# Layer 1's softmax pass of a graph network on one core: all feature weighting and a quarter of the copying out on GpSimd, the per-head scales in PSUM

## The reference, cut to what matters

```python
h = (x @ W_lin + b_lin).reshape(N, HEADS, EMB)
ee = (edge_attr @ W_edge + b_edge).reshape(-1, HEADS, EMB)
x_i = h[src]
x_j = h[dst] + ee
alpha = (x_i * att_i).sum(-1) + (x_j * att_j).sum(-1)
alpha = jnp.where(alpha >= 0, alpha, NEG_SLOPE * alpha)
amax = jax.ops.segment_max(alpha, src, num_segments=N)
e = jnp.exp(alpha - amax[src])
denom = jax.ops.segment_sum(e, src, num_segments=N)
alpha = e / (denom[src] + 1e-16)
messages = x_j * alpha[:, :, None]
out = jax.ops.segment_sum(messages, src, num_segments=N)
```

## Time and profile before

| what | value |
|---|---|
| median of 3 runs | 10118.95 us (10105.5 to 10135.94) |
| the profiled execution | 10148.2 us, span 10146.4 us |
| DVE busy over the span | 6640.8 us, 65% |
| ACT busy over the span | 4732.1 us, 47% |
| POOL busy over the span | 6862.4 us, 68% |
| the pass that is changed, first to last record | 4650.8 to 5342.9 us |

### The profile page before, as it was taken

One profiled execution on the slowest core, in us unless ns is written; L12 is line 12 of the kernel. 1 busy time (PEld: TensorE's weight loads), 2 busy tenths in 40 slices (PEclk: granted clock), 3 DMA queues, 4 the chain that ended last, 5 costly groups with the idle time before them and its releaser, 6 DMA issues. The chain is left out here.

```text
span 10146.4 us, 93449 instructions
## 1 busy us (share of the span) xinstructions
PE 2857.7 (28%) x19432; PEld 2389.4 (24%) x19432; DVE 6640.8 (65%) x9437; ACT 4732.1 (47%) x6635; POOL 6862.4 (68%) x6738
## 2 busy tenths in 40 slices
PE   1112587873000000000003566666664400000002
PEld 1111477773000000000003344444443200000002
DVE  7888777775122232226994688888886677777775
ACT  1111477772121111115991577777774344444442
POOL 6767777775677777775443777777775277777774
PEclk9999877775555555555556677777776655555555
DMA  3332322222233332324662444444442477777773
GB/s 103 101 94 89 87 72 80 76 92 32 95 120 112 105 116 102 116 98 181 261 249 63 114 140 134 140 134 140 134 140 77 150 237 236 236 237 236 236 237 104
DMA packets 722785, 1395.94 MB, mean 138 GB/s; under 512 B 409551, under 2 KB 439452, under 8 KB 715094
## 3 DMA queue, kind: packets, MB, share of 16 engines
q0 software_dynamic: 287072, 587.19, 21.1%
q1 hardware_dynamic: 406786, 639.32, 18.9%
q10 hardware_dynamic: 28852, 168.65, 4.6%
HBM read 827.48 MB, written 602.51 MB: 141 GB/s over the span
## 5 line engine op out<-in xcount | busy, mean ns | idle before, releaser
L823 POOL DMA_INDIRECT l_rows<-in_x,l_idx x1568 | 1638.1, 1045 | 685.5 <-issue 446.8
L2484 POOL DMA_INDIRECT l_rows<-table,l_idx x1568 | 1485.8, 948 | 660.8 <-issue 471.8
L1964 POOL DMA_INDIRECT l_rows<-h,l_idx x1568 | 1528.1, 975 | 571.3 <-issue 445.0
L1304 POOL DMA_INDIRECT rows<-l_rows,l_idx x1568 | 1503.6, 959 | 524.5 <-issue 496.5
L1999 PE MATMUL l_made<-l_kv_w,l_rows_t 128*128 128x256 f32 x3136 | 1081.3, 501 | 768.0 <-ACT l_kv L2029 452.6
L2560 ACT ACTIVATE l_lifted<-l_rows,l_up 128x256 f32<-128x256 f32 x1568 | 639.5, 460 | 1031.3 <-DMA l_rows<-table,l_idx 1031.3
L1999 PEld LDWEIGHTS l_made<-l_kv_w,l_rows_t 128*128 128x128 f32 x3136 | 753.3, 257 | 971.4 <-issue 842.7
L1260 ACT COPY l_rows<-l_run 128x1792 f32<-128x1792 f32 x56 | 191.6, 3421 | 1561.5 <-POOLq L88 1520.8
L1293 DVE TENSOR_TENSOR l_rows<-l_run,l_weights_ps 128x56 f32<-128x56 f32 x56 | 12.0, 215 | 1296.5 <-POOLq L88 1296.2
L1737 PE MATMUL l_wide<-l_diag,l_ones 128*128 128x384 f32 x4 | 3.3, 928 | 2957.3 <-DVEq L1767 2957.3
L1737 PEld LDWEIGHTS l_wide<-l_diag,l_ones 128*128 128x128 f32 x4 | 1.0, 311 | 2958.2 <-DVEq L1767 2958.2
(11 more groups left out here) (400 smaller groups left out, 12352.7 us busy)
## 6 DMA issues: line engine op xcount, KB each, us to landing
sums<-l1s_out ACTq DMA_DIRECT2D x56, 1988.0 KB, 6.6
sums<-l_out SPq DMA_DIRECT2D x112, 924.0 KB, 4.4
spread<-zeros SPq DMA_DIRECT2D x28, 3612.0 KB, 12.7
l_spread<-spread SPq DMA_DIRECT2D x112, 903.0 KB
l1s_rows<-rows SPq DMA_DIRECT2D x56, 1008.0 KB, 6.1
spread<-zeros SPq DMA_DIRECT2D x56, 938.0 KB
l_spread<-spread SPq DMA_DIRECT2D x56, 938.0 KB, 10.9
sums<-l_out ACTq DMA_DIRECT2D x56, 896.0 KB
```

The source lines that it names most:

```text
L823: pool.indirect_dma_start(rows[:, b, t], None, a["x"], bass.IndirectOffsetOnAxis(ap=idx[:, b, t:t + 1], axis=0)) \
L1304: pool.indirect_dma_start(g["rows1_d"], bass.IndirectOffsetOnAxis(ap=idx[:, b, t:t + 1], axis=0), rows[:, b, t], None).then_inc(sent[b], 16)
L1964: pool.indirect_dma_start(rows[:, c.r, t, 0:C], None, g["h2_d"], bass.IndirectOffsetOnAxis(ap=idx[:, c.r, t:t + 1], axis=0)).then_inc(got[ ...
L2484: pool.indirect_dma_start(rows[:, b, t], None, g["table3_d"], bass.IndirectOffsetOnAxis(ap=idx[:, b, t:t + 1], axis=0)) \
```

## The change

In `source_order_sums`:

- `weigh` on POOL (now L1508) does all 140 columns of a half, as two tensor_tensor instructions of 70 x 28 elements (L1513), into the SBUF tensor that held scales and weighed values before. It waits for the exponentials and for `scanned[n]` of the chunk before; `begun` is gone.
- `copy_out` on POOL (L1518) is new: it copies the last 35 of the 140 sums of a half into `outb` (L1521). ACT copies the other 105 (L1560).
- DVE's `sums` keeps only a column copy of 140 elements (L1490, from SBUF to SBUF) and two scans of 2030 elements, one for each head (L1496).
- The scales of each head lie in a PSUM tensor of their own, written by ACT once for each half and head (L1554), with semaphores `scale_ready` and `scale_used`.
- `scores` is unchanged, and so are SP's loads (the count they wait for is raised by one engine, not two) and the stores, which now also wait for POOL's copy.

```diff
-        LOW = F // 2
-        weighed_low = s.ps("l1s_weighed_low", [P, 2 * 512])[:, 0:LOW * (T + 1)].rearrange("p (f t) -> p f t", t=T + 1)
-        scale_high = s.ps("l1s_scale_high", [P, 6 * 512])[:, 0:(W - LOW) * (T + 1)].rearrange("p (f t) -> p f t", t=T + 1)
+        COPIED = W * 3 // 4
+        scale_ps = [s.ps(f"l1s_scale{h}", [P, 4 * 512])[:, 0:F * (T + 1)].rearrange("p (f t) -> p f t", t=T + 1) for h in range(H)]
+        weighed, run_all = scale, run[:].rearrange("p n h f t -> p n (h f) t")
...
                 def sums(c):
-                    b = c.b
-                    wait(v, exp_ready[b], c.h + 2)
                     for n in range(PARTS):
-                        at = slice(n * T, (n + 1) * T)
-                        v.tensor_tensor(weighed_low[:, :, 1:].rearrange("p f t -> p t f"), rows[:, b, at, 0:LOW],
-                                        exp[:, b, 1, 0, at].unsqueeze(2).to_broadcast([P, T, LOW]), ALU.mult).then_inc(rows_used[b][n], 1)
-                        v.tensor_copy(weighed_low[:, :, 0], run_all[:, 1 - n, 0:LOW, T]).then_inc(begun, 1)
-                        wait(v, low_ready[n], c.at + 1)
+                        wait(v, weighed_ready[n], c.at + 1)
+                        v.tensor_copy(weighed[:, n, :, :, 0], run[:, 1 - n, :, :, T])
                         wait(v, copied[n], c.at + 1)
+                        wait(v, out_copied[n], c.at + 1)
                         v.drain()
...
+                        for h in range(H):
+                            wait(v, scale_ready[h], c.at * PARTS + (n + 1))
+                            last = v.tensor_tensor_scan(run[:, n, h].rearrange("p f t -> p (f t)"), scale_ps[h].rearrange("p f t -> p (f t)"),
+                                                        weighed[:, n, h].rearrange("p f t -> p (f t)"), 0.0, ALU.mult, ALU.add)
+                            last.then_inc(scale_used[h], 1)
+                        v.drain().then_inc(scanned[n], 1)
...
                 def weigh(c, n):
                     at = slice(n * T, (n + 1) * T)
                     wait(pool, exp_ready[c.b], c.h + 2)
-                    if not (isinstance(c.g, int) and c.at == 0 and n == 0):
-                        wait(pool, begun, c.at * PARTS + n)
...
+                    wait(pool, scanned[n], c.at + 1)
+                    for h in range(H):
+                        last = pool.tensor_tensor(weighed[:, n, h, :, 1:].rearrange("p f t -> p t f"), rows[:, c.b, at, 0:F],
+                                                  exp[:, c.b, 1, h, at].unsqueeze(2).to_broadcast([P, T, F]), ALU.mult)
+                    last.then_inc(rows_used[c.b][n], 1)
+                    pool.drain().then_inc(weighed_ready[n], 1)
+
+                def copy_out(c, n):
+                    wait(pool, scanned[n], c.at + 2)
+                    wait(pool, stored[n], (c.at + 1) * 16)
+                    pool.tensor_copy(outb[:, n, :, COPIED:W].rearrange("p t w -> p w t"), run_all[:, n, COPIED:, 1:])
+                    pool.drain().then_inc(out_copied[n], 1)
+
+                def turn(c, after):
+                    copy_out(c, 0)
+                    if after:
+                        weigh(after, 0)
+                    copy_out(c, 1)
+                    if after:
+                        weigh(after, 1)
...
-                def low(c, n):
...
-                def high(c, n):
...
+                def scales(c, n, h):
+                    wait(act, scale_used[h], c.at * PARTS + (n + 1))
+                    nc.scalar.copy(scale_ps[h][:, :, 1:], exp[:, c.b, 0, h, n * T:(n + 1) * T].unsqueeze(1).to_broadcast([P, F, T])).then_inc(scale_ready[h], 1)
...
-                    nc.scalar.copy(outb[:, n, :, 0:W].rearrange("p t w -> p w t"), run[:, n].rearrange("p h f t -> p (h f) t")[:, :, 1:])
+                    nc.scalar.copy(outb[:, n, :, 0:COPIED].rearrange("p t w -> p w t"), run_all[:, n, 0:COPIED, 1:])
...
                 def turn(c, after):
-                    high(c, 1)
+                    scales(c, 1, 0)
+                    scales(c, 1, 1)
                     if after:
                         exponentials(after)
                     store(c, 0)
+                    send(c, 0)
                     if after:
-                        low(after, 0)
-                        high(after, 0)
+                        scales(after, 0, 0)
+                        scales(after, 0, 1)
                     store(c, 1)
-                    if after:
-                        low(after, 1)
+                    send(c, 1)
```

More of the change, by code:

```diff
@@ L1435, in source_order_sums @@
         rows_used = [two(f"rows_used{b}_") for b in range(2)]
-        low_ready, high_ready, scanned, copied, stored = (two(n) for n in ("low_ready", "high_ready", "scanned", "copied", "stored"))
-        set_up, begun, high_weighed = sem("l1s_set_up"), sem("l1s_begun"), sem("l1s_high_weighed")
+        scanned, copied, out_copied, stored, weighed_ready = (two(n) for n in ("scanned", "copied", "out_copied", "stored", "weighed_ready"))
+        set_up, scale_ready, scale_used = sem("l1s_set_up"), two("scale_ready"), two("scale_used")
         flat = lambda t: t.rearrange("p h t -> p (h t)")
@@ L1444, in _ @@
                     for n in range(PARTS):
-                        wait(sp, rows_used[c.b][n], (c.h + 1) * 2)
+                        wait(sp, rows_used[c.b][n], c.h + 1)
                         sp.dma_start(rows[:, c.b, n * T:(n + 1) * T].rearrange("p t w -> p (t w)"),
@@ L1454, in _ @@
                     for n in range(PARTS):
-                        v.sem_inc(rows_used[b][n], 2)
+                        v.sem_inc(rows_used[b][n], 1)
                     v.sem_inc(exp_ready[b], 1)
@@ L1458, in _ @@
                     v.sem_inc(copied[b], 1)
+                    v.sem_inc(out_copied[b], 1)
                     v.sem_inc(stored[b], 16)
-                v.memset(scale_high, 0.0)
+                    v.sem_inc(scale_used[b], 1)
+                    v.memset(scale_ps[b], 0.0)
                 v.drain().then_inc(set_up, 1)
@@ L1522, in weigh @@
-                    pool.drain().then_inc(high_weighed, 1)
-                pool.wait_ge(set_up, 1)
-                for r in range(UNROLL):
[L1526 to L1531, removed]
+                    wait(pool, scanned[n], c.at + 1)
+                    for h in range(H):
+                        last = pool.tensor_tensor(weighed[:, n, h, :, 1:].rearrange("p f t -> p t f"), rows[:, c.b, at, 0:F],
+                                                  exp[:, c.b, 1, h, at].unsqueeze(2).to_broadcast([P, T, F]), ALU.mult)
@@ L1533, in _ @@
+                pool.wait_ge(set_up, 1)
+                weigh(Chunk(0, 0), 0)
+                weigh(Chunk(0, 0), 1)
+                with pool.Fori(0, NB // UNROLL - 1) as q:
+                    for r in range(UNROLL):
+                        turn(Chunk(q, r), Chunk(q, r + 1) if r + 1 < UNROLL else Chunk(q + 1, 0))
+                for r in range(UNROLL):
+                    turn(Chunk(NB // UNROLL - 1, r), Chunk(NB // UNROLL - 1, r + 1) if r + 1 < UNROLL else None)
             @block.scalar
@@ L1557, in store, with send @@
                     wait(act, stored[n], (c.at + 1) * 16)
-                    nc.scalar.copy(outb[:, n, :, 0:W].rearrange("p t w -> p w t"), run[:, n].rearrange("p h f t -> p (h f) t")[:, :, 1:])
+                    nc.scalar.copy(outb[:, n, :, 0:COPIED].rearrange("p t w -> p w t"), run_all[:, n, 0:COPIED, 1:])
                     nc.scalar.copy(outb[:, n, :, W:W + H], top[:, c.r, :, at].rearrange("p h t -> p t h")).then_inc(copied[n], 1)
+                def send(c, n):
                     wait(act, copied[n], c.at + 2)
+                    wait(act, out_copied[n], c.at + 2)
                     act.dma_start(sums_v[:, bass.ds((c.at * PARTS + n) * wide, wide)], outb[:, n].rearrange("p t w -> p (t w)")).then_inc(stored[n], 16)
                 exponentials(Chunk(0, 0))
-                low(Chunk(0, 0), 0)
-                high(Chunk(0, 0), 0)
-                low(Chunk(0, 0), 1)
+                scales(Chunk(0, 0), 0, 0)
+                scales(Chunk(0, 0), 0, 1)
                 def turn(c, after):
-                    high(c, 1)
+                    scales(c, 1, 0)
+                    scales(c, 1, 1)
                     if after:
```

15 lines of the change are left out of this document (removed).

## The result

| | before | changed |
|---|---|---|
| median | 10127.44 us (4 runs, 10105.5 to 10151.37) | 10312.84 us (4 runs, 10295.15 to 10317.21) |
| ratio | | 1.0175, 95% interval 1.015 to 1.02 |
| the profiled execution | 10148.2 us | 10317.21 us |

What follows compares the result with a forecast made beforehand. DVE was taken to set the pace at 23.80 us a chunk. 26 x 7.6 for held scores, +8 and -5 at the edges gave +201 us; put onto the median, 10320 us (+2.0%), range 10215 to 10400.

Steps and rivals of the forecast that it cites:

- clean period: Time a chunk in the changed pass if DVE waited for nobody: 21.8 to 21.9 us.
- C: Duration of POOL's new copy of 980 elements a half, taken as 1.9 us.
- T: End of a chunk's second scans, when POOL's second burst is let go and DVE goes on to the scores.
- What the first burst leaves over: POOL work let go by the first half's end and still running when the second scans end: 0.8 us.
- The hold: In the scores, POOL instructions make DVE's SBUF operations wait one by one; period 31.4 us against 23.8, +7.6 a chunk.
- how many of the twelve score instructions pass POOL's gaps: One DVE instruction, perhaps two, passes each gap; about four of twelve done at T + 10.5, scores ending at T + 13.1.
- The sign of being wrong: If score lines 1468 to 1471 keep 0.16 to 0.24 us, the mechanism is wrong.
- The edges: Start and end of the pass: +8 us up to and after the first sums, -5 us at the last chunk.
- Rival 1: Score operations with two tensor inputs are not held: 2.8 us less a chunk, -73, 10247 us; chance 0.18.
- Rival 2: No hindrance of weight at a steady pace, clean period of 21.8 holds: faster, 10062 us; chance 0.10.
- Rival 3: Three or more DVE instructions pass each gap: +0.7 to +3 us a chunk, 10137 to 10197 us; chance 0.07.
- Rival 4: POOL's copy is far from 1.9 us: at 1.0, 10276 us; at 4.1, 10434; no separate chance given.

Runs made afterwards that it cites:

- e2_fence_18: Kernel of e1_fence with POOL copying out 18 of the 140 columns instead of 35, ScalarE 122; ratio to the kernel before 0.9969.
- e1_fence: Changed kernel plus one wait: POOL starts its second burst of a chunk only after VectorE's scores are done; ratio to the kernel before 0.9991.
- e4_spare_tt: Kernel before plus one POOL tensor_tensor of 1960 elements on a spare tensor during each chunk's scores; 11654.88 us against 11560.83 for the kernel before.
- e5_spare_set: e4_spare_tt with the extra POOL instruction made a memset of 3920 elements; 10136.30 us against 10150.98 for the kernel before.
- e3_no_pool_copy: Changed kernel without POOL's copy, ScalarE copying all 140 columns, no wait added; 11729.31 us against 11560.83 for the kernel before.
- e6: e2_fence_18 plus a wait at the pass's start: POOL's second-half weighting follows chunk 1's scores; ratio to the kernel before 0.9972.

## Why the prediction was right, and where it was off

The direction, the mechanism and the bound were right. That 10320 lies within 8 us of the measured 10312.84 is in part luck: +201 was forecast, the medians are 185 apart and the profiled executions 169, and the median of the kernel before had moved up by 8 us with a fourth run.

- **The bound and the clean period.** DVE set the pace, and the sum of its own work gave 21.8 to 21.9 us a chunk. e2_fence_18, where POOL is nearly out of the way, has 22.16.
- **What moved to POOL and what it takes.** C was taken as 1.9 us and is 1.92; two weightings in 7.5 are 7.45. POOL's burst was to end at T + 10.5, and it ends at T + 10.57 (4987.11 - 4976.54). What the first burst leaves over was put at 0.8 and is 0.64. Its path was only half right: the first burst's weightings follow POOL's copy, which ends at 4969.40, but also wait for the exponentials, which end in the same moment (the `<-ACT l1s_exp L1549` at 4969.76). So a shorter copy would not have shortened what is left over.
- **The hold.** It was read from two rows at the beginning of the pass. The steady pace of the changed kernel, e1_fence (taken away by time alone) and e4_spare_tt (put into the kernel before) show it. The forecast stated the rule with POOL instructions that read SBUF; for copies that was too narrow, since a memset held one as well (e4_spare_tt, e5_spare_set).
- **The term that was mis-sized: how many of the twelve score instructions pass POOL's gaps.** The forecast let about four be done when POOL's last instruction ends, with 2.5 us from 1473 on still to come. In the chunk shown the ninth, 1480, ends with it. Four pass in the one gap of 0.3 us in which POOL drains and waits for its semaphores, since the copies start only 0.07 to 0.15 us apart, and 1475 passes in the next. So 0.8 us were left when 1482 started, and the scores end at T + 11.6, not 13.1. The halves take the rest of the 30.16, about 18.5, not 18.3. The period is 30.16, not 31.4, and 26 x 1.24 = 32 us is the distance between +201 and the +169 of the profiled executions.
- **The sign of being wrong was badly chosen.** The forecast said that the mechanism is wrong if 1468 to 1471 keep 0.16 to 0.24 us. In 20 of 26 chunks they do, because they pass in the gap, and yet the hold is there: it falls on 1473, 1477 and 1480. So in most chunks the cost hung on the case that two-tensor operations are held, to which the forecast had given a rival with a chance of 0.18, and that case carried more of it than the sum, with its holds among the copies, let see.
- **The edges** were +8 and -5. Measured are +6.9 and, behind the start of the last scores, +2.9, in which the 26th period's 6.4 is contained: -3.5 to the end of the last scan, -5.8 to the end of ScalarE's last copy.
- **Rival 1** (two-tensor operations pass) fell: 1473, 1477 and 1480 stand for 1.4, 3.4 and 2.7 us in the mean, and e4_spare_tt shows such an operation held with nothing else changed. The forecast chose right there, though on thin ground: no row of before showed such an operation under POOL. **Rival 2** fell with it. **Rival 3** has the gaps right, where more than one passes, and their effect wrong: instructions that pass a gap run into the next POOL instruction all the same, as long as twelve are more than fit. **Rival 4** didn't arise, but its reason was wrong on the low side: e3_no_pool_copy, with no copy at all, has 0.6 us left over at T, so C doesn't count twice below 1.9. The estimate of 0.84 us from the Trainium skill ("GPSIMD Engine Reference", section 3.1) isn't met by this copy with its turned writes, which takes 1.92, and the measurement decides.

## What to carry to other kernels

Work moved from VectorE to an idle GpSimd is free only while VectorE's operations at that moment are of a kind that GpSimd doesn't hold. Short SBUF operations that come in a row are the worst place for it: here a row that takes 3.3 us by itself took 11.4, as long as the burst and a little more. Look for a short operation with a duration far above its siblings' in the trace, ask which moment releases GpSimd's work, and let it wait until the row of short operations is over, so that it runs beneath the long ones that don't meet it. Then size its share by its free time less that stretch: in this pass the wait alone brought the kernel back to where it was, and with a smaller copy it became 0.3% faster.

## What the runs showed of the hardware

- A held operation ends with the GpSimd instruction that held it, and in a gap of 0.3 us as many as four short ones got through behind it; between two weightings issued back to back only the held one got through. In four records a held tensor_scalar stands through both weightings (6.6 us in e1 and e6, 7.2 in e2, 7.4 in e3), though the instruction behind it starts about when the first one ends; why, no run shows.
- The scan with one operand in PSUM is held in no run here: 112 of them lie between 4358 and 4387 ns in the changed kernel, with POOL at work under those of every second half.
- GpSimd's copy with turned writes takes 1.92 us for 980 elements and 1.07 for 504, so 1.8 ns an element, as many as a product of two tensors takes from 980 to 1960 elements (1.86, from 1995 and 3814 ns). Its memset takes 3.36 us for 3920 elements and 1.73 for 1960, so 0.83 ns an element.
- ScalarE needs the same 1.8 ns an element for the turned copy (5348 ns for 2940) and 0.8 for the broadcast of the scales, from 1786 ns for 1960 elements and, also in the kernel before, 973 for 980:

```profile
L1551 ACT COPY l1s_scale_high<-l1s_exp 128x980 f32<-128x980 f32 x56 | 54.5, 973 | 0.0
```
